# Softmax normalisation of an attention unit moved beside its exponential, units drained at each head pair, and the expert input cast before its transposes

## What is computed

```
# x: 4 x 2048 x 2048 f32, 16 heads of 128
q, k, v = x @ Wq, x @ Wk, x @ Wv
scores  = q @ k.T, causal mask, / sqrt(128)
ctx     = softmax(scores) @ v
x = layernorm(x + ctx @ Wo)
# feed-forward on flat = x: 2 shared and 16 routed experts, D 2048, F 1408
out    = flat + sum over shared of relu(flat @ w1) @ w2
s      = sigmoid(flat @ centroids.T) + bias
gating = s where s is among its row's top 4, else 0, divided by the row's sum
out   += sum over routed experts j of gating[:, j] * (relu(flat @ w1[j]) @ w2[j])
x = layernorm(x + out)
```

## Time and profile before

| | |
|---|---|
| median of the runs shown | 4772.26 us (2 runs: 4593.78 and 4950.74) |
| the profiled execution | 4461.9 us |
| its span, slowest core | 4460.4 us |
| spans of its eight cores | 4427.2 to 4460.4 us |
| TensorE busy | 3885.3 us (87%) |
| VectorE, ScalarE busy | 1007.8 us, 796.8 us |

### The profile page before, as it was taken

The page is one execution under the profiler, slowest core; times in us unless marked ns, Lnnn a source line. Parts: engine busy times, 40 slices in busy tenths (PEclk is TensorE's granted clock), DMA queues, the critical chain, the costliest instruction groups (busy, mean ns, idle before and its releaser), DMA issues.

```text
span 4460.4 us, 48368 instructions; the slowest of 8 cores (4427.2 to 4460.4 us)
## 1 busy us (share of the span) xinstructions
PE 3885.3 (87%) x20016; PEld 1930.9 (43%) x20016; DVE 1007.8 (23%) x2242; ACT 796.8 (18%) x1212; POOL 223.3 (5%) x427
## 2 busy tenths in 40 slices
PE   2875785676686999999999999999999999999997
PEld 2543553443454444444444444444444444444443
DVE  2224214313314331111211211121121111112112
ACT  0233324323324310011001001001100100100114
POOL 0000000000000010000001001000000100100000
PEclk8887887787686999999999999999999999999998
DMA  8101101110115063255246236425524632642552
GB/s 147 29 1 29 29 1 29 29 17 12 29 20 132 11 104 66 45 98 90 41 78 104 48 57 104 72 42 95 93 40 76 104 53 51 104 69 45 95 95 76
DMA packets 65129, 274.46 MB, mean 62 GB/s; under 512 B 7406, under 2 KB 7918, under 8 KB 60816
## 3 DMA queue, kind: packets, MB, share of 16 engines
q0 software_dynamic: 60704, 253.99, 33.7%
q1 hardware_dynamic: 4208, 17.37, 1.2%
HBM read 516.84 MB, written 8.39 MB: 118 GB/s over the span
## 4 chain that ended last, share of the span: by engine, by line
PE 77%; DMA 7%; DVE 6%; issue 4%; ACT 4%; DVEq 0%; ACTq 0%; POOLq 0%; POOL 0%; SPq 0%
PE PP L957 30%; PE PP L876 26%; PE PP L523 5%; PE PP L503 5%; DMA ar<-w1x 4%; PE PP L468 3%; DVE ar L331 3%; PE PP L427 3%; PE PP L606 3%; PE PP L310 2%; DMA ar<-xs 2%; ACT ar L412 1%; DVE ar L323 1%; DMA ar<-xo 1%; PE PP L395 1%
## 5 line engine op out<-in xcount | busy, mean ns | idle before, releaser
L957 PE MATMUL PP<-ar 128*128 128x512 bf16 x6336 | 1392.9, 383 | 47.5 <-DVE ar L935 45.1
L876 PE MATMUL PP<-ar 128*128 128x512 bf16 x6336 | 1386.1, 379 | 24.9 <-DMA ar<-w1x 17.5
L957 PEld LDWEIGHTS PP<-ar 128*128 128x128 bf16 x6336 | 623.3, 99 | 816.6 <-issue 87.0
L876 PEld LDWEIGHTS PP<-ar 128*128 128x128 bf16 x6336 | 610.8, 98 | 797.0 <-issue 81.9
L890 ACT ACTIVATE ar<-PP,b_sb 128x512 bf16<-128x512 f32 x396 | 250.7, 684 | 2531.1 <-PE PP L876 2531.1
L980 DVE SCALAR_TENSOR_TENSOR ar<-PP,ar 128x512 f32<-128x512 f32 x576 | 357.6, 683 | 1032.8 <-PE PP L957 1022.3
L427 PE MATMUL PP<-ar 128*128 128x128 bf16 x1152 | 119.8, 271 | 342.4 <-ACT ar L412 204.5
L902 DVE TENSOR_TENSOR ar<-ar 128x1024 bf16<-128x1024 bf16 x176 | 121.9, 693 | 1121.0 <-ACT ar L890 1121.0
L427 PEld LDWEIGHTS PP<-ar 128*128 128x128 bf16 x1152 | 92.9, 121 | 369.6 <-issue 369.6
L523 PE MATMUL PP<-ar 128*128 128x256 bf16 x2048 | 230.6, 277 | 0.0
L503 PE MATMUL PP<-ar 128*128 128x512 bf16 x1024 | 228.2, 386 | 0.0
(11 more groups left out here) (100 smaller groups left out, 1217.9 us busy)
## 6 DMA issues: line engine op xcount, KB each, us to landing
ar<-w1x POOLq DMA_DIRECT2D x198, 512.0 KB, 6.3
ar<-w2x POOLq DMA_DIRECT2D x198, 512.0 KB, 8.3
ar<-wqkv POOLq DMA_DIRECT2D x8, 2048.0 KB, 16.4
ar<-wqkv POOLq DMA_DIRECT2D x8, 1024.0 KB, 22.3
ar<-xs POOLq DMA_DIRECT2D x4, 2048.0 KB, 37.1
ar<-wo POOLq DMA_DIRECT2D x2, 4096.0 KB, 41.8
ar<-xo SPq DMA_DIRECT2D x8, 1024.0 KB, 9.9
out<-ar SPq DMA_DIRECT2D x16, 512.0 KB, 3.3
```

Of the source, the lines that this page charges most:

```text
L876: e.matmul(PA[:, bank * 512:(bank + 1) * 512], W1c[pp][:, dc * 128:(dc + 1) * 128], xhat[:, dc * 1024 + nt * 512: dc * 1024 + (nt + 1) * 512],
L957: e.matmul(PP[:, bank * 512:(bank + 1) * 512], H_sb[:, fc * 1024 + ti * 128: fc * 1024 + (ti + 1) * 128], W2c[:, fc * 2048 + (bank % 4) * ...
```

## The change

Four things are done.

1. **Normalisation.** It moves from behind the next unit's front to right behind the exponential of its own unit. VectorE waits for the exponential, takes the reciprocal, and then one engine alone scales all kc columns: ScalarE for even units, VectorE for odd ones. (16 units a group, so a unit's parity is that of i.)
2. **Back.** It runs two units behind. All batches of a unit are evicted by one engine: VectorE for even units, ScalarE for odd ones. There are two `p_sb` buffers instead of three.
3. **Drain.** The units left over are finished at the end of their own group, before the next Q projection.
4. **Expert input.** After all 8 row blocks are normalised, ScalarE (even blocks) and VectorE (odd blocks) write them as bf16, halved, into `u_bf`, which lies where the Wo weights were. Then 16 batches of 8 bf16 blocks are transposed and VectorE copies each out.

```
 def emit_unit_exp(g, jl, i, up, mstat):
+    (exponential as before, then)
+    sb.wait("vector", "ac", sc_state["free"][up])
+    sb.do("vector", reciprocal(linv_sp[up], lsum_sp[up]), "dv", 1)
+    if up == 0:
+        mr = sb.mark("dv")
+        sb.wait("scalar", "dv", mr)
+        sb.do("scalar", activation(p_sb[up][:, 0:kc], p_sb[up][:, 0:kc], AF.Copy,
+                                   bias=0.0, scale=linv_sp[up]), "ac", 1)
+        mpn = ("ac", sb.mark("ac"))
+    else:
+        sb.vchain(tensor_scalar(p_sb[up][:, 0:kc], p_sb[up][:, 0:kc],
+                                linv_sp[up], None, ALU.mult))
+        mpn = ("dv", sb.mark("dv"))
+    return mpn
-def emit_unit_norm(ent):            (removed)

 def emit_unit_back(...):
-    ev_eng = "vector" if (bi + up) % 2 == 0 else "scalar"
+    ev_eng = "vector" if up == 0 else "scalar"

 for g in range(8):
     (Q projection)
-    if norm_pend["e"] is not None: emit_unit_norm(norm_pend["e"])
-    while pend: emit_unit_back(pend.pop(0))
     (K and V projections)
     for jl in range(2):
         for i in range(8):
+            up = unit_par
             mstat = emit_unit_front(g, jl, i, up)
-            if norm_pend["e"] is not None: emit_unit_norm(norm_pend["e"])
-            if len(pend) >= npar: emit_unit_back(pend.pop(0))
-            ent["exp_ac"] = emit_unit_exp(g, jl, i, up, mstat)
+            if len(pend) >= 2: emit_unit_back(*pend.pop(0))
+            mpn = emit_unit_exp(g, jl, i, up, mstat)
+            pend.append((g, jl, i, up, mpn))
+            unit_par ^= 1
+    while pend: emit_unit_back(*pend.pop(0))

 (expert input)
-for ti in range(8):
-    sb.wait("tensor", "ac", ln1_ap_ac[ti])
-    for half in range(2):
-        8 x e.transpose(PTf[half][...], x_tm[ti][:, dc * 128:(dc + 1) * 128], identf_sb)
-        e.tensor_scalar(xh3[...], PTf[half]..., 0.5, None, ALU.mult)
+sb.wait("scalar", "ac"); sb.wait("scalar", "pe", wo_pe)
+sb.wait("vector", "ac", ln1_all_ac); sb.wait("vector", "pe", wo_pe)
+for ti in range(8):
+    even: scalar activation(u_bf[ti block], x_tm[ti], AF.Copy, scale=0.5)
+    odd:  vector tensor_scalar(u_bf[ti block], x_tm[ti], 0.5, None, ALU.mult)
+sb.wait("tensor", "ac", ubf_ready_ac); sb.wait("tensor", "dv", ubf_ready_dv)
+for dc in range(16):
+    8 x e.transpose(PTb[...], u_bf[block b, columns dc], ident_sb)
+    vector tensor_copy(xhat[:, dc * 1024:(dc + 1) * 1024], PTb[...])
```

More of the change, by code:

```diff
@@ L377, in emit_unit_back @@
+        return mpn
+    def emit_unit_back(g, jl, i, up, mpn):
         nonlocal pt_free_pe, ctx_evac_ac
-        g, jl, i, up = ent["g"], ent["jl"], ent["i"], ent["up"]
         kc = kcount(i)
         nkb = kc // 128
-        hA, mpnA, mpnB = ent["mpn"]
-        ev_marks = []
-        for bi, b0 in enumerate(range(0, nkb, 8)):
+        ev_eng = "vector" if up == 0 else "scalar"
+        ev_sem = "dv" if up == 0 else "ac"
+        sb.wait("tensor", *mpn)
+        for b0 in range(0, nkb, 8):
             bpar = (b0 // 8) % 2
+            sb.wait("tensor", *ptb2_free[bpar])
@@ L415, in emit_unit_back @@
             ptb2_free[bpar] = (ev_sem, sb.mark(ev_sem))
-            ev_marks.append((ev_sem, sb.mark(ev_sem)))
         p_free_pe[up] = sb.mark("pe")
-        for m_ in ev_marks:
-            sb.wait("tensor", *m_)
+        sb.wait("tensor", ev_sem, sb.mark(ev_sem))
         if i == 0:
@@ L657, in build_nc @@
     wo_pe = sb.mark("pe")
[L659 to L676 removed]
+    ln1_all_ac = sb.mark("ac")
@@ L681, in build_nc @@
                                    0.5, None, ALU.mult)),
                   "dv", 1)
-            ptf_free[half] = [("dv", sb.mark("dv"))]
+    ubf_ready_ac = sb.mark("ac")
+    ubf_ready_dv = sb.mark("dv")
+    if dbg:
+        mln_ac = sb.mark("ac")
+        sb.wait("sync", "ac", mln_ac)
+        for ti in range(8):
+            sb.dma("sync",
+                   (lambda e, ti=ti: e.dma_start(out=dbg_u[:, ti * 2048:(ti + 1) * 2048],
+                                                 in_=x_tm[ti][:, :])),
+                   pool="store")
+        sb.wait_all("vector", sb.dma_total_marks("store"))
@@ new lines, in build_nc @@
+    sb.wait("tensor", "ac", ubf_ready_ac)
+    sb.wait("tensor", "dv", ubf_ready_dv)
+    for dc in range(16):
+        bpar = dc % 2
+        sb.wait("tensor", *ptb2_free[bpar])
+        for b in range(8):
+            sem = "pe" if b == 7 else None
+            sb.do("tensor",
+                  (lambda e, dc=dc, b=b, bpar=bpar:
+                   e.transpose(PTb[:, bpar * 1024 + b * 128: bpar * 1024 + (b + 1) * 128],
+                               u_bf[:, b * 2048 + dc * 128: b * 2048 + (dc + 1) * 128], ident_sb[:, :])),
+                  sem, 1)
+        m = sb.mark("pe")
+        sb.wait("vector", "pe", m)
+        sb.do("vector",
+              (lambda e, dc=dc, bpar=bpar:
+               e.tensor_copy(xhat[:, dc * 1024:(dc + 1) * 1024], PTb[:, bpar * 1024: bpar * 1024 + 1024])),
+              "dv", 1)
+        ptb2_free[bpar] = ("dv", sb.mark("dv"))
```

141 lines of the change are left out of this document (47 added, 94 removed).

## The result

The changed kernel takes 4393.9 us in the median, its profiled execution 4392.0 us (span 4390.5). In some executions, whatever the kernel, the cores of one die run at a lower granted clock and the time is some per cent longer, so all ratios here are over the others. The ratio to the kernel before is 0.988, with a 95% interval of 0.985 to 0.991: 1.2% faster.

A forecast was written before the change was run, and what follows sets the result against it. No engine is full; a chain hopping between engines bounds the units. Seven groups -4, last group -4, expert input +2 make -6 us on 4461.9: 4456 us, range 4405 to 4620.

The forecast's parts named there:

- VectorE's chain: Attention units: VectorE waits for each exponential before the next front, 35.7 us a head.
- F + E + 0.4: Even unit's time: VectorE front (1.20 to 3.58 us), exponential with sum read-out (0.60 to 2.09), 0.4 for hops and reciprocal.
- The step from 35.7 to 36.1: First head of a group: raised to 36.1 us because TensorE can be later than VectorE in even units.
- TensorE's longer queue in even units: Even units: VectorE's eviction follows the front, delaying contexts and scores; i = 6 5.95 us against 5.3, i = 4 4.5 against 4.3.
- Turn of the heads and drain: Second head's first units 4.8 and 7.3 us; last front to Q projection 14.65 us, at the lower clock.
- rival (a): Drain and head turns get warm, giving 4 us a group, about 4424 us in all; chance 0.10.
- Q itself I leave at 16.2: Q projection after each group's units: time unchanged at 16.2 us.
- The reference: Whole kernel before: the profiled execution's 4461.9 us, from which the forecast change of -6 us was counted.
- 87.4 against 86.8: A group's units with left-over units, before against after: a gain of 0.6 us a group, 4 for seven.
- Part 3: Drain at group end: 14.65 us; losing the Q projection's cover costs some 5 us, partly there already.
- Part 4: Expert input: casts to 1546.6, then 13.7 us of transposes to 1560.5; cost 2.0 us, bounds 0 to +5.
- the case I had given 0.86: Whole kernel: time the same within about 2%, 90 us, counted as no change; chance 0.86.

The follow-up runs named there:

- The gap experiment: Changed kernel with two idle ScalarE copies, which TensorE waits for, ahead of seven groups' Q projections; Q took mean 15.6 us on core 1 instead of 13.8.

## Why the prediction was wrong

**VectorE's chain** (F + E + 0.4, and 0.5 and the scaling in odd units): right. Unit i = 7 6.80 for 6.9, and the first head 35.65 for 36.1. (The step from 35.7 to 36.1 is less than the excesses given for i = 4 and i = 6, 0.2 and 0.65, which would make it 36.5.) The scaling of 2048 columns: right to 0.01.

**TensorE's longer queue in even units** was right in kind; i = 6 took 5.8 us (672.7 to 678.5) for 5.95.

**Turn of the heads and drain**: the mechanism was right, the size wrong. I priced the matmuls there at the lower clock; at the turn they ran at 1.00, and the last 16 of the drain too. 4.8 and 7.3 became 3.7 and 6.0, 14.65 became 13.6. Units and drain: 83.5 us a group for 86.8, 7 x 3.3 = 23 us. This was rival (a), which I had given 0.10, and its "against" took the mean clock of a whole stretch, 0.61, for the level of its densest part.

**"Q itself I leave at 16.2"**: the step that failed outright. Q took 13.8, 7 x 2.4 = 17 us. I had seen that it starts cold, and that the change puts other work ahead of it, and did not ask what the clock would be behind that work. The gap experiment shows the link: with 4.9 us of standstill ahead of it, Q starts at clock 0.50 again and takes 15.6 us.

**The reference**: 28.5 us of the 64 between forecast and profiled execution were core 3's own. I had the spans of all cores (4427 to 4460) and used the longest, without laying its stages beside those of another core. The page's clock row would not have told me, as core 1's has as many low slices. Group 3 of that core, on which I built the comparison, also took 103.6 us where core 1's groups took 104.1, another 3 us. Against these 72 us in all stand 8 that the change took and I had not forecast: 2 ahead of the experts and 6 in them.

**My reading of the old order** hid the rest. I compared sums, 87.4 against 86.8, and did not ask why the old units were slow although no engine waited for an exponential. Their chain runs over ScalarE's share of the normalisation, which stood still for 3.18 us in the unit above. This explains the comparison, not the miss of the time: the measured old durations held it already.

**Part 3** cost more than it gave, as I had it in sign: I put the lost cover at about 5 us a group, partly made up; undoing it gives 1.3 to 3. **Part 4**: 2.0 us forecast up to the router, 31.6 us instead of 29.1 to 29.4 from the last output matmul to the first centroid matmul, so 2.2 to 2.5; not foreseen was the cold start of the output projection (its first five matmuls take 2.29 us; on core 1 before it started at clock 1.00, on core 3 at 0.50), 1.5 us more than on core 1, and that of the first expert matmuls. The rule of the Trainium skill (TensorE: Matmul & The Clock Gate, Part 4: PE-mode transpose), by which transposes would not bring the full clock, does not hold here either: the pass began at clock 0.50 and reached 1.00 with nothing but transposes on TensorE.

The change stayed under 2%, the case I had given 0.86, but by the width of that case and not by my sum, which had 0.1%. The range failed at its lower end, which had no room for both clock terms together with a better reference.

## What to carry to other kernels

When work is deferred so that it does not wait, look at every engine that gets a share of it: a small operation that waits for another engine holds up all that stands behind it in its queue (3.18 us in a unit of the kernel before), and here the same deferred order gave 1.003 with half of a scaling on ScalarE and 0.975 with all of it on VectorE. Sum against a core that agrees with its neighbours, and check each stage of the reference against its repetitions. And a matmul stage that follows a changed one has a new price: ask what TensorE did just before it starts.

## What the runs showed of the hardware

- After a gap of 4.9 us ahead of dense matmuls, TensorE ran them at clock 0.50 for about 5.5 us and at 1.00 from then on. Behind the changed kernel's drain, whose gaps reach 3 us, it started at 1.00.
- Transposes alone raised TensorE's clock: 0.50 over the first 2.3 us of the expert input's pass, 1.00 from 4.3 us after its start.
- VectorE casts 2048 f32 columns from SBUF to bf16 in 1.16 us; 1024 from PSUM had taken 1.18. The Trainium skill (VectorE: DVE Perf Modes, The perf-mode tier table) gives 1.23 us for a `tensor_scalar` over 2048 fp32 elements in SBUF, and the trace agrees within 6%.
- Two cores of one execution, on the same code, can differ by 28.5 us, with clock 0.83 against 1.00 over the same 400 matmuls.
